# A fourth PSUM bank for attention scores and one shared bank for most outputs, in a fused transformer kernel on one core

## What is computed

```python
q = l2norm(q) * qs;  k = l2norm(k) * ksc
q, k = rotary_xpos(q, k)
sim = einsum('bhwid,bhwjd->bhwij', bq, bk)      # bk: previous window and own
sim = where((i < j) | (i > j + 128) | (j == -1), -max, sim)
attn = softmax(sim)
out = einsum('bhwij,bhwjd->bhwid', attn, bv)
x = x + out.reshape(b, n, 512) @ wo
...
h = layernorm(shift_token(x)) @ w1 + b1
a, g = split(h, 2);  x = x + (a * gelu(g)) @ w2 + b2
```

## Time and profile before

| | us |
|---|---|
| median of three runs | 792.92 |
| the profiled execution | 791.66 |
| span in its profile | 789.9 |
| PE busy (matmul) | 722.1 |
| DVE / ACT / POOL busy | 531.9 / 481.3 / 436.0 |

### The profile page before, as it was taken

The page is one execution under the profiler, slowest core; times in us unless marked ns, Lnnn a source line. Parts: engine busy times, 40 slices in busy tenths (PEclk is TensorE's granted clock), DMA queues, the critical chain, the costliest instruction groups (busy, mean ns, idle before and its releaser), DMA issues.

```text
span 789.9 us, 17103 instructions
## 1 busy us (share of the span) xinstructions
PE 722.1 (91%) x4952; PEld 599.1 (76%) x4952; DVE 531.9 (67%) x1486; ACT 481.3 (61%) x1291; POOL 436.0 (55%) x592
## 2 busy tenths in 40 slices
PE   6988964999999999999999899999999999999967
PEld 5777753787878787878787777878787878787847
DVE  2798897286757575858575955757575757575732
ACT  2343622468585858585857684757575757585742
POOL 1433454465575656656565565748484747474722
PEclk9999985799999999999999999999999999999988
DMA  7444330451101010101010001010101010101000
GB/s 210 153 146 155 102 68 29 146 199 44 41 2 40 0 40 0 40 0 40 9 31 13 27 1 54 2 54 0 53 0 53 0 53 0 53 0 41 1 28 13
DMA packets 32786, 38.36 MB, mean 49 GB/s; under 512 B 8476, under 2 KB 22896, under 8 KB 32752
## 3 DMA queue, kind: packets, MB, share of 16 engines
q1 hardware_dynamic: 32752, 37.95, 15.1%
HBM read 29.55 MB, written 8.39 MB: 48 GB/s over the span
## 4 chain that ended last, share of the span: by engine, by line
PE 57%; issue 7%; DVE 7%; ACT 5%; POOL 4%; DMA 1%; ACTq 0%; SPq 0%; DVEq 0%; POOLq 0%
PE ps L423 34%; PE ps L625 4%; PE ps L584 3%; PE ps L611 3%; POOL pr L1389 3%; PE ps L602 2%; PE ps L596 2%; PE ps L629 2%; ACT pr L870 2%; PE ps L518 2%; PE ps L613 1%; PE ps L612 1%; PE ps L416 1%; DVE hT_lo L1140 1%; ACT hT_hi L909 1%
## 5 line engine op out<-in xcount | busy, mean ns | idle before, releaser
L1389 POOL TENSOR_SCALAR pr<-pr,rl 128x128 f32<-128x128 f32 (+1 forms) x256 | 107.7, 434 | 78.2 <-DVE rl L1173 77.5
L870 ACT ACTIVATE pr<-sm,mn 128x128 f32<-128x128 f32 (+1 forms) x256 | 113.6, 448 | 15.4 <-DVE mn L1167 14.6
L423 PE MATMUL ps<-hT_hi,w_hi 128*128 128x256 f32 (+1 forms) x352 | 105.4, 299 | 3.6 <-DVE hT_lo L1140 1.4
L1167 DVE CUSTOM_DVE_ANT_0 sm<-ps,wmask 128x128 f32<-128x128 f32 (+1 forms) x256 | 80.1, 355 | 35.0 <-PE ps L602 30.3
L423 PE MATMUL ps<-hT_hi,w_lo 128*128 128x256 f32 (+1 forms) x352 | 100.3, 285 | 0.0
L423 PE MATMUL ps<-hT_lo,w_hi 128*128 128x256 f32 (+1 forms) x352 | 99.4, 282 | 0.0
L1355 POOL TENSOR_TENSOR rn<-ss,nhalf 128x16 f32<-128x16 f32 x32 | 95.9, 2998 | 2.7
L830 ACT ACTIVATE sqb<-ps 128x512 f32<-128x512 f32 x64 | 37.9, 595 | 89.9 <-PE ps L423 83.6
L423 PE MATMUL ps<-wqkv_hi,yT_hi 128*128 128x512 f32 x192 | 80.1, 417 | 7.7 <-DVE arena L1012 5.1
L423 PE MATMUL ps<-wqkv_lo,yT_hi 128*128 128x512 f32 x192 | 77.2, 402 | 0.0
L423 PE MATMUL ps<-wqkv_hi,yT_lo 128*128 128x512 f32 x192 | 77.2, 402 | 0.0
(11 more groups left out here) (156 smaller groups left out, 2132.7 us busy)
## 6 DMA issues: line engine op xcount, KB each, us to landing
arena<-x SPq DMA_DIRECT2D x16, 256.0 KB, 3.6
ystream<-arena SPq DMA_DIRECT2D x16, 256.0 KB, 2.0
y_next<-ystream SPq DMA_DIRECT2D x16, 256.0 KB, 2.7
y_res<-ystream SPq DMA_DIRECT2D x16, 256.0 KB, 2.6
arena<-L_ffn_w SPq DMA_DIRECT2D x6, 640.0 KB
arena<-ctx SPq DMA_DIRECT2D x8, 256.0 KB, 3.9
arena<-mask_BxSxS_ik SPq DMA_DIRECT2D x8, 256.0 KB, 2.7
xmid<-arena SPq DMA_DIRECT2D x8, 256.0 KB, 2.0
```

What stands on the lines that cost most here:

```text
L423: last = mm(out, lhsT(a), rhs(b), start=(start and i == 0), stop=(stop and i == 2))
L870: A(pr[:, h % NS, a:b], sm[:, h % NS, a:b], ACT.Exp, bias=mn[:, h, t:t + 1], scale=-1.0, accum_out=ls[:, h, t:t + 1]).then_inc(e_done, 1)
L1167: V.tensor_tensor_reduce(sm[:, h % NS, a:b], bank(h % SB)[:, a:b], wmask[:, a:b], 1.0, -NEG, ALU.add, ALU.min, mn[:, h, t:t + 1]).then_inc ...
L1389: G.tensor_scalar(pr[:, h % NS, a:b], pr[:, h % NS, a:b], rl[:, h, t:t + 1], 1.0, ALU.mult, ALU.mult).then_inc(pn_done, 1)
```

## The change

The scores get four banks, 0, 1, 2 and 6, in turn. The outputs of pairs 0, 1 and 2 go to bank 5 one after the other, that of pair 3 to bank 3. PE's order, ACT's and DVE's are changed with it, and the waits that guard the banks.

```diff
-    NS, SB = 4, 3
+    NS, SB = 4, 4
+        def scores_bank(h):
+            return bank((0, 1, 2, 6)[h % SB])
+
+        def output(pair):
+            return bank(3 if pair == PAIRS - 1 else 5)[:, 0:S]
...
             def bias_products(l):
-                pe.wait_ge(mn_done, T * (HEADS * NB * l + HEADS - 2))
+                pe.wait_ge(mn_done, T * (HEADS * NB * l + HEADS - 1))
...
                     elif 0 in parts:
-                        wait(pe, pT_done, HEADS * s)
+                        wait(pe, o_done, PAIRS * s)
...
                         if h >= SB:
                             pe.wait_ge(mn_done, T * (HEADS * s + h - SB + 1))
+                        elif h == SB - 1 and lf is not None:
+                            pe.wait_ge(u_raw, HC * s)
...
                 def weighted(pair):
-                    b = bank(5 + pair % 2)
+                    b = output(pair)
                     pe.wait_ge(pT_done, HEADS * s + 2 * pair + 2)
-                    if pair >= 2:
-                        pe.wait_ge(o_done, PAIRS * s + pair - 1)
-                    elif lf is not None:
+                    if 0 < pair < PAIRS - 1:
+                        pe.wait_ge(o_done, PAIRS * s + pair)
+                    elif pair == 0 and lf is not None:
                         pe.wait_ge(u_done, HC * s)
...
                     scores_both(0)
-                    downs(5)
+                    downs(2)
+                    scores_own(1)
+                    scores_both(1)
+                    downs(8)
                     for h in range(HEADS + 1):
-                        if h in (0, 1, 3):
-                            scores_own((h + 3) // 2)
-                            scores_both((h + 3) // 2)
-                        if h == 0:
-                            downs(7)
                         if h < HEADS:
                             tr_probs(h)
+                        if h in (0, 2):
+                            scores_own(2 + h // 2)
+                            scores_both(2 + h // 2)
                         if isinstance(s, int) and s in (0, NB) and h == HEADS - 1:
                             bias_products(la)
-                        downs(min(10, 7 + (h + 1) // 2))
+                        downs({1: 9, 3: 10, 5: 11}.get(h, 0))
                         if h and h % 2 == 0 and h < HEADS:
                             weighted(h // 2 - 1)
...
# ScalarE
                     for h in range(HEADS):
+                        if h in (3, 5):
+                            heads_out((h - 3) // 2)
                         if h + 2 < HEADS:
                             exps(h + 2)
                         probs_T(h)
-                        if h >= 3 and h % 2:
-                            heads_out((h - 3) // 2)
+                        if h == HEADS - 1:
+                            heads_out(PAIRS - 2)
...
# VectorE
                         if h + 3 < HEADS:
                             row_min(h + 3)
-                        if h >= 4 and h % 2 == 0:
-                            low_oT((h - 4) // 2)
+                        if h in (3, 5):
+                            low_oT((h - 3) // 2)
```

More of the change, by code:

```diff
@@ L593, in scores_own @@
                             pe.wait_ge(mn_done, T * (HEADS * s + h - SB + 1))
+                        elif h == SB - 1 and lf is not None:
+                            pe.wait_ge(u_raw, HC * s)
                     for h in (2 * pair, 2 * pair + 1):
                         r = slice(h % 2 * DH, h % 2 * DH + DH)
-                        mm(bank(h % SB)[:, 0:P], qT[r, pair, 0:P], kT[r, pair, 0:P], start=True, stop=True)
+                        mm(scores_bank(h)[:, 0:P], qT[r, pair, 0:P], kT[r, pair, 0:P], start=True, stop=True)
                 def scores_both(pair):
@@ L601, in scores_both @@
                         r = slice(h % 2 * DH, h % 2 * DH + DH)
-                        mm(bank(h % SB)[:, P:3 * P], qT[r, pair, P:S], kT[r, pair, :], start=True, stop=True)\
+                        mm(scores_bank(h)[:, P:3 * P], qT[r, pair, P:S], kT[r, pair, :], start=True, stop=True)\
                             .then_inc(s_mm2, 1)
@@ L880, in heads_out @@
                     wait(act, wo_mm, s)
-                    A(oT[0][:, pair, :], bank(5 + pair % 2)[:, 0:S], ACT.Copy).then_inc(o_high, 1)
+                    A(oT[0][:, pair, :], output(pair), ACT.Copy).then_inc(o_high, 1)
                 if isinstance(s, int) and s == NB:
@@ L1159, in low_oT @@
                     dve.wait_ge(o_high, PAIRS * s + pair + 1)
-                    V.tensor_tensor(oT[1][:, pair, :], bank(5 + pair % 2)[:, 0:S],
+                    V.tensor_tensor(oT[1][:, pair, :], output(pair),
                                     oT[0][:, pair, :].bitcast(F32), ALU.subtract).then_inc(o_done, 1)
@@ L1166, in row_min @@
                     for t, (a, b) in enumerate(((0, P), (P, 3 * P))):
-                        V.tensor_tensor_reduce(sm[:, h % NS, a:b], bank(h % SB)[:, a:b], wmask[:, a:b], 1.0,
+                        V.tensor_tensor_reduce(sm[:, h % NS, a:b], scores_bank(h)[:, a:b], wmask[:, a:b], 1.0,
                                                -NEG, ALU.add, ALU.min, mn[:, h, t:t + 1]).then_inc(mn_done, 1)
```

## The result

The changed kernel takes 795.78 us (median of 8, 794.77 to 796.78) against 791.13 us for the kernel before in the same session (8 runs): a ratio of 1.0055, 95% interval 1.0039 to 1.0072. So it is slower by 0.4 to 0.6%, by the medians 4.7 us here and 3.4 us in e11. The forecast was 795.5 us, made of +3.4 us on a kernel before that was taken between 791.66 and 792.92 us.

The account below looks back on a forecast made before the run. PE was taken to bound the step nearly everywhere, attention's end hanging on ACT's exps 6 and 7. 14 steps by 0.2, 0.55 and 0 gave +3.4 us, 795.0 to 796.3, predicted 795.5 us; 8-in-10 range 789.5 to 800.

Parts of the forecast that it names:

- sum of +3.4 us: Whole kernel: 14 steps by 0.2 us, 0.55 us for the last step and 0 for step 0.
- Scores sooner give nothing on PE: Attention start: earlier scores bring head 2's row minimum some 0.4 us sooner, but nothing on PE waits for it.
- ACT's gap before e(2): ACT ahead of the exps of head 2: its 0.41 us gap was to close with the sooner row minimum.
- w(0) at 8.2 us: PE's weighted outputs of pair 0: start 8.2 us after the step's first scores instead of 7.53.
- ACT stands 0.87 us, exps 5 0.91, exps 7 and transpose 7 0.54 later: ACT waits about 0.87 us at heads_out(0), delaying exps 5 by 0.91 us, exps 7 and PE's transpose 7 by 0.54.
- The tail gives 0.34 us back: PE behind transpose 7: with one down moved ahead, 1.98 us to the wo projection instead of 2.32.
- +0.2 us in each of 14 steps: Middle steps: the wo projection starts 0.2 us later in each, walked on step 4.
- DVE's low_oT of the last pair keeps its distance: DVE near the step's end: the last pair's subtraction stays 0.42 us behind its copy, costing the wo projection nothing.
- The output bank's waits are covered: PE's outputs of pairs 1 and 2: waits on low_oT in the shared bank covered by about a microsecond, cost nothing.
- Step 0 nothing, last step +0.55: Step 0: delay mostly covered by the weight wait, 0 give or take 0.4 us; last step: no tail gain, +0.55.
- ACT's second copy: Slower rival: ACT also stalls at heads_out(1), the step costs 0.5 us, about 799 us; chance 0.33.
- The faster rival: ACT takes heads_out(0) without standing still, only the tail's 0.35 us a step counts, 787.7 us; chance 0.10.

Follow-up runs that it names:

- e11: The changed kernel measured again in another session, nothing altered: 794.29 us, ratio 1.0044 to the kernel before.
- e8: Changed kernel with PE's scores of pair 1 put back behind five downs instead of two: 798.86 us, ratio 1.0079 to the kernel before.
- e2: Changed kernel with heads_out(0) and (1) behind exps 5 and 7, low_oT behind row_sum 5 and 7: 788.00 us, ratio 0.9958 to the kernel before.
- e3: Changed kernel with PE's scores of pair 3 put back behind the outputs of pair 0: 787.54 us, ratio 0.9956 to the kernel before.
- e7: Changed kernel with one down call moved back behind transpose 7: 799.79 us, ratio 1.0086 to the kernel before.
- e4: Changed kernel with DVE's low_oT of the last pair ahead of add_down, except steps 0 and 8: 792.43 us, ratio 1.0014 to the kernel before.
- e1: Changed kernel with ACT's and DVE's orders of before, banks and PE's order staying changed: 796.13 us, ratio 1.0060 to the kernel before.
- e5: Kernel before with DVE's low_oT of the last pair ahead of add_down, except steps 0 and 8: 791.63 us, ratio 0.9983.
- e10: Kernel before with DVE's low_oT(3) and low_yT both ahead of add_down, except steps 0 and 8: 789.55 us, ratio 0.9981.

## Why the prediction was right, and where it was not

Its time was met within 0.3 us, and its sum of +3.4 us lies in the intervals of both measurements. That it came so near is in part luck. The kernel before was taken 0.5 to 1.8 us slower than it ran beside the changed one, where the difference was 4.7 us. And of the 2.8 us counted for 14 even steps the trace shows 3.12, but 0.16 of them in eight steps and 2.96 in six. The mechanism of ACT's stall and of PE's shorter tail is right.

- *Scores sooner give nothing on PE.* Nearly right: 27 us less of DVE's wait, transpose 0 no earlier (4.75 us after the first scores in both). But transpose 2, which POOL held before, comes 0.11 us sooner, and e8 puts what the early scores of pair 1 are worth at 0.17 us a step. The minimum of head 2 came 0.20 us sooner (3.77 for 3.97 us), not 0.4, and ACT's gap before e(2) shrank from 0.41 to 0.22 us and did not close.
- *w(0) at 8.2 us.* 8.09. The switch from scores to outputs, for which I had no row, costs nothing (306.26 to 307.12 is 0.86 us, as to a down), and a transpose straight behind a down is 0.06 us shorter ahead of scores.
- *ACT stands 0.87 us, exps 5 0.91, exps 7 and transpose 7 0.54 later.* The mechanism is right (e2 and e3 each remove it), the size was over: 0.69 us between pT(2)'s effective end (307.00 + 0.37) and the copy, exps 5 later by 0.78, exps 7 by 0.39, transpose 7 by 0.38. Some 0.14 us of it come from w(0) above.
- *The tail gives 0.34 us back.* Right: 1.96 us from transpose 7 to the projection through wo (1.98 predicted, 2.32 before), and e7 takes it away again, 0.36 us.
- *+0.2 us in each of 14 steps.* Wrong, and this is the step that failed: +0.02 in layer 0, where transpose 7 is 0.38 us later and the tail gives 0.36 back, and +0.47 in layer 1 (0.65 in step 9). I walked step 4 and counted it 14 times, with "DVE's low_oT of the last pair keeps its distance". That holds where add_down is one operation. In layer 1 it is two, low_oT(3) was already 0.74 us behind its copy's start there (0.42 us in step 4), and moved with transpose 7, not with w(3). e4 shows it: 0.37 us of the 0.47 go, in those steps alone, and w(3) is 0.09 us later there in any case.
- *The output bank's waits are covered.* Right for the changed kernel: w(1) was released by pT(3), at 10.80 us. The rule of the Trainium skill (Perfetto Trace Analysis, Matmuls) that independent matmul groups should rotate through different banks, to let the evacuation of one overlap the next, agrees with e1: once the copies were late, one bank held w(1) for 0.63 us. In the changed kernel itself the shared bank held nothing at w(1).
- *Step 0 nothing, last step +0.55.* +0.5 in step 0 and +0.41 at the end in this execution (w(3) at 15.41 us, 15.05 before, which is the 0.36 us by which transpose 7 came later). Neither total stands clear of chance: step 0 is the same program in the kernel before, e5 and e10 and took 57.05, 55.39 and 57.32 us, and the end is the same in e5 and e10 and took 47.22 and 48.39.
- *The rivals.* ACT's second copy did not stall in the changed kernel (310.83 follows pT(4) at once). The faster rival had 0.35 us a step for a kernel whose ACT isn't held, and 787.7 us. e2 is such a kernel, and its 788.0 us are near by chance: its steps are 0.67 us under the kernel before in layer 0 and 0.20 in layer 1. In step 4 transpose 7 comes 0.30 us sooner than before (13.68 for 13.98), which the rival left out, and the tail gives its 0.36 as well.

## What to carry to other kernels

An instruction moved forward on an in-order engine must be ready when its turn comes: compare when its input is there with when its place in the queue comes up, and if the input is later, put the next ready instruction first. A shorter wait of an engine that isn't the bound (27 us of it here) is worth only what of it arrives at the engine that is. And when steps of a loop differ by a single operation, walk one of each kind: the same 0.4 us of delay at transpose 7 cost next to nothing in one layer and 0.47 us in the other.

## What the runs showed beyond it

Steps 0 and 8, which load weights and make bias products, vary between executions and kernels by more than the change moves them: step 0 took 55.39 to 58.48 us and step 8 48.41 to 50.79 us in the thirteen profiles of this study. For step 8 the granted clock goes with it. In the changed kernel and in e2, from the first scores of step 8 to those of step 9:

```profile
458.15:507.04 48.89, 45.40 (x324) 38.43 (x323) 31.39 (x81) 31.24 (x80) 30.70 (x36) 0.93 0.07 23
```

```profile
454.93:504.66 49.73, 47.37 (x323) 40.55 (x322) 30.20 (x81) 31.18 (x80) 31.80 (x36) 0.90 0.06 22
```

The mean clock of the step was 0.93 of full speed in the kernel before, the changed kernel, e5, e10 and e11, where the step took 48.41 to 48.97 us, and 0.90 in the other eight, where it took 49.64 to 50.79. What set the clock I have not tested. Step 0 had 0.78 to 0.80 in all thirteen, so the mean clock does not explain its spread, and the cause is open. Part of e2's account stays open with it: against the kernel before, its steps 1 to 7 and 9 to 14 are 5.7 us shorter, its median gave 3.6, and its steps 0 and 8 were 2.1 us longer in the profile.
